# Dense products of a transformer row computed in 64-row TensorE tiles, two banks at a time, with their halves placed around the score products

## What is computed

```python
xn = layernorm(x)                                     # no affine part
q, k, v = split_heads(xn @ qkv_w + qkv_b)             # 16 heads of 16
attn = softmax(q @ k.T * 0.25)
a = (attn @ v) @ proj_w + proj_b
h = silu(xn @ wg.T) * (xn @ wu.T)                     # wg, wu: 768 x 256 integers / 127
return x + a + h @ wd.T                               # wd: 256 x 768 integers / 127
```

## Time and profile before

| | |
|---|---|
| median of 3 runs | 620.43 us (619.53 to 620.57) |
| the profiled execution | 619.78 us, of which the span from first to last instruction is 618.0 us |
| PE, busy | 599.4 us, 97% of the span |
| DVE, ACT, POOL, busy | 494.6, 372.3, 173.0 us |
| TensorE clock granted | full in all of the span's slices |

### The profile page before, as it was taken

How to read it: one execution, slowest core, us unless ns; L and a number is a source line. 1 busy time by engine, 2 the same in 40 slices (tenths; PEclk the granted TensorE clock), 3 DMA queues, 4 the chain that set the end, 5 groups by cost and what they waited for, 6 DMA issues and landing times.

```text
span 618.0 us, 10940 instructions
## 1 busy us (share of the span) xinstructions
PE 599.4 (97%) x3594; PEld 327.1 (53%) x3594; DVE 494.6 (80%) x652; ACT 372.3 (60%) x482; POOL 173.0 (28%) x181
## 2 busy tenths in 40 slices
PE   7888999999999999999999999999999999999896
PEld 6655445555555555555555455555555555554353
DVE  5898887788887887888877888878878788778752
ACT  3545765675566665766556655666657665566563
POOL 3215134220622224321342206222152212222210
PEclk9999999999999999999999999999999999999999
DMA  8680192114622176012822137221760118210201
GB/s 285 226 136 3 69 236 56 53 37 140 169 53 52 35 209 149 17 36 102 235 56 52 35 133 174 51 52 35 197 162 14 41 69 232 61 53 3 69 2 38
DMA packets 38364, 59.11 MB, mean 96 GB/s; under 512 B 6080, under 2 KB 21440, under 8 KB 38336
## 3 DMA queue, kind: packets, MB, share of 16 engines
q1 hardware_dynamic: 38336, 58.74, 35.1%
HBM read 37.23 MB, written 20.97 MB: 94 GB/s over the span
## 4 chain that ended last, share of the span: by engine, by line
PE 90%; DVE 5%; ACT 3%; issue 1%; DMA 0%; POOL 0%; DVEq 0%; ACTq 0%; POOLq 0%
PE dense L948 38%; PE o_bank L938 20%; PE st_bank L907 17%; PE s_bank L924 11%; DVE neg_max L705 2%; ACT probs L582 2%; PE dense L962 1%; PE dense L979 1%; DMA xn<-in_L_attn_x 0%; DVE gated L733 0%; DVE hid L741 0%; PE dense L1006 0%; ACT gated L621 0%; DVE w_gl L757 0%; ACT xn_th L590 0%
## 5 line engine op out<-in xcount | busy, mean ns | idle before, releaser
L582 ACT ACTIVATE probs<-st_bank 128x1024 f32<-128x1024 f32 x250 | 256.2, 1025 | 206.4 <-PE st_bank L907 202.5
L705 DVE TENSOR_REDUCE neg_max<-s_bank 128x2 f32<-128x1024 f32 x250 | 305.4, 1222 | 69.3 <-PE s_bank L924 67.2
L938 PE MATMUL o_bank<-probs,v_ones 128*32 128x512 f32 x1024 | 136.4, 604 | 0.1
L907 PE MATMUL st_bank<-q_stack,k_stack 50*128 50x512 f32 x500 | 125.0, 496 | 4.1 <-ACT probs L582 3.9
L517 POOL TENSOR_TENSOR hid_tl<-hid,hid_th 128x512 fp32r<-128x512 f32 x48 | 61.9, 1289 | 188.8 <-ACT hid_th L647 188.8
L907 PEld LDWEIGHTS st_bank<-q_stack,k_stack 50*128 50x128 f32 x500 | 46.6, 183 | 121.9 <-ACT probs L582 84.7
L924 PE MATMUL s_bank<-k_stack,q_stack 48*128 48x512 f32 x500 | 110.1, 436 | 0.7 <-DVE neg_max L705 0.7
L924 PEld LDWEIGHTS s_bank<-k_stack,q_stack 48*128 48x128 f32 x500 | 47.0, 185 | 23.1 <-DVE neg_max L705 20.8
L550 POOL TENSOR_TENSOR resid<-resid,p_bias 128x256 f32<-128x256 f32 x32 | 22.5, 735 | 101.5 <-DMA resid<-in_L_attn_x 101.5
L526 POOL TENSOR_TENSOR o_norm<-o_blocks,inv_sum 128x256 f32<-128x256 f32 x31 | 19.3, 621 | 93.7 <-DVE inv_sum L770 93.5
L938 PEld LDWEIGHTS o_bank<-probs,v_ones 128*32 128x32 f32 x1024 | 20.4, 108 | 45.8 <-issue 43.8
(11 more groups left out here) (120 smaller groups left out, 683.0 us busy)
## 6 DMA issues: line engine op xcount, KB each, us to landing
q_spread<-qk_parts SPq DMA_DIRECT2D x16, 512.0 KB, 3.2
k_spread<-qk_parts SPq DMA_DIRECT2D x16, 512.0 KB, 3.5
q_stack<-q_spread SPq DMA_DIRECT2D x64, 128.0 KB, 3.0
k_stack<-k_spread SPq DMA_DIRECT2D x64, 128.0 KB, 3.2
q_stack<-q_spread SPq DMA_DIRECT2D x64, 64.0 KB, 3.2
k_stack<-k_spread SPq DMA_DIRECT2D x64, 64.0 KB, 3.1
resid<-in_L_attn_x SPq DMA_DIRECT2D x8, 512.0 KB, 4.3
xn<-in_L_attn_x SPq DMA_DIRECT2D x7, 512.0 KB, 3.4
```

The lines of the kernel that those rows point to most:

```text
L582: nc.scalar.activation(probs[:, s % 2, 2 * half:2 * half + 2, :], transposed_bank(row, s, half)[:, :, :], ACT.Exp, scale=SCALE).then_inc(e ...
L705: nc.vector.tensor_reduce(neg_max[:, g % 2, :, NT * pair + qt], score_bank(row, half)[:, :, :], AX_X, ALU.max, negate=True).then_inc(max_d ...
L907: done = nc.tensor.matmul(transposed_bank(row, s, half)[:, r, :], k_stack[rows, pair, P * kt:P * (kt + 1)], q_stack[rows, pair, :], start= ...
L938: done = nc.tensor.matmul(o_bank[32 * j:32 * (j + 1), :], v_ones[:, kt, 8 * (g // 2) + 2 * j + g % 2, :], probs[:, (s - 1) % 2, j, :], sta ...
```

## The change

`dense` becomes one tensor of three banks, and each entry of the table names its banks. From row 0 on every dense product is cut along its contraction into array rows 0 to 63 and 64 to 127, the two row tiles that the scores use, and works on two banks: in a first half, tile 0 adds into bank A while tile 1 adds into bank B; in the second half the tiles are swapped. up and gate of one index are made together, and q and k of index 1; the others fill two banks with 256 columns each (two token tiles of v, proj and down; two halves of the tokens for q 0 and k 0). The first half of a product stands behind `scores_t` of the second pair of the step before (for up/gate one pair of matmuls ahead of `scores`, the rest behind it), the second half behind `scores_t` of the first pair of its step, or behind `scores` where it is long (down, q and k 1). The transposes (xn, max) still use the whole array.

ACT alone empties the banks of xn, q, k, up, v and max. xn, q and k go whole into a float32 tile (`whole`, on the place of `raw_d`); ACT makes the high part from there and POOL the low part. up is copied to `hid` by ACT, POOL multiplies it with the gated value, ACT and POOL split that product. The low part of the maxima is made by POOL. DVE keeps the maxima, the gate, down and proj (now two tiles of down at once). `resid` is stored and loaded in two halves. Row -1 keeps whole-array products; its last chunk is v 0 in place of gate 4.

```diff
+    (0, 0, "up", 4, 0, (2,)), (0, 0, "gate", 4, 0, (0,)),
+    (1, 0, "v", 1, 0, (1, 2)),
+    (2, 0, "up", 5, 0, (1,)), (2, 0, "gate", 5, 0, (0,)), (2, 1, "max", 1, 0, (2,)),
...
+    (5, 0, "q", 0, 1, (1, 2)),
+    (6, 0, "k", 0, 1, (0, 1)), (6, 1, "max", 2, 0, (2,)),
+    (7, 0, "proj", 1, -1, (0, 1)),
+    (8, 0, "q", 1, 1, (2,)), (8, 0, "k", 1, 1, (0,)),
+    (9, 0, "down", 0, 0, (1, 2)),
...
+    (12, 0, "up", 1, 1, (2,)), (12, 0, "gate", 1, 1, (1,)),
...
+            def half_product(spec, swap, first, last):
...
+                for n, (ready, (a, b, k)) in enumerate(terms):
+                    if not first <= n < end:
+                        continue
+                    if ready is not None and swap == 0:
+                        pe.wait_ge(*ready)
+                    for r in range(2):
+                        h = (r + swap) % 2
+                        rows = slice(HALF * r, HALF * (r + 1))
+                        done = nc.tensor.matmul(banks[h], stationary(h, a, k)[rows], moving(h, b, k)[rows],
+                                                start=swap == 0 and n == 0, stop=swap == 1 and n == len(terms) - 1,
+                                                tile_position=(HALF * r, 0))
+                return done, end == len(terms)
...
+            def end_product(row, chunk, exact):
+                pe.wait_ge(half_made, products_up_to(row, chunk))
+                done, _ = half_product(spec_of(row, chunk, exact), 1, 0, None)
+                done.then_inc(dense_done, len(made_together(row, chunk)))
...
             def step(row, exact):
                 for s in range(STEPS):
                     chunks(row, s, 0, exact)
-                    pairs(row, s, 0)
+                    here = product_at(row, s)
+                    if here and s == 0:
+                        begin_product(row, here, exact, 0)
+                    if row.has(0):
+                        scores_t(row, s, 0)
+                    if here and not long_product(here):
+                        end_product(row, here, exact)
+                    if pair_ahead(row, s, 0):
+                        scores(row, s, 0)
+                    if here and long_product(here):
+                        end_product(row, here, exact)
...
-                    if not after_scores(row, s):
-                        pairs(row, s, 1)
+                    if row.has(0) and not after_scores(row, s):
+                        scores_t(row, s, 1)
+                    ahead = product_at(row, s + 1)
+                    between = ahead and ahead[2] == "up"
+                    if between:
+                        begin_product(row, ahead, exact, 0, 1)
+                    if pair_ahead(row, s, 1):
+                        scores(row, s, 1)
+                    if ahead:
+                        begin_product(row, ahead, exact, 1 if between else 0)
...
+            def hidden_product(row, chunk):
+                m = chunk[3]
+                (up,) = [c for c in chunks_of(row.like) if c[2:4] == ("up", m)]
+                wait_freed(pool, row, up)
+                wait_freed(pool, row, chunk)
+                nc.gpsimd.tensor_tensor(gated[:, m % 2, :], gated[:, m % 2, :], hid[:, m % 2, :],
+                                        ALU.mult).then_inc(hid_product, 1)
...
+                elif kind == "up":
...
+                    nc.scalar.activation(halves(hid[:, i % 2, :]), bank, ACT.Copy,
+                                         scale=0.5 * QUANT ** 3).then_inc(act_free, 1)
...
+            def split_into_high(row, chunk, n):
...
+                nc.scalar.activation(high, whole[:, WHOLE_AT[kind, i], :], ACT.Copy).then_inc(split_high, 1)
```

More of the change, by code:

```diff
@@ L139, in rows_of, with count @@
     step(Row(ROWS, ROWS))
-PER_ROW = {kind: sum(c[2] == kind for c in STEADY) for kind in ALL}
-def count(row, kinds, chunk=None, kind=None, index=None):
+def count(row, which, chunk=None, kind=None, index=None):
     like = row.like
@@ L333, in pair_ahead, with number @@
+        def number(row, kind, index):
+            return count(row, lambda like, k: k == kind, kind=kind, index=index)
         def pair_ahead(row, step, half):
@@ L483, in step @@
                     load_stack(row, 3)
+                if row.like == ROWS:
+                    for tiles in (slice(0, 2), slice(2, 3), slice(3, 4)):
+                        sp.wait_ge(last_added, tiles.stop)
+                        sp.dma_start(out_rows[row.at - 1, :, tiles],
+                                     resid[:, tiles, :]).then_inc(out_done[tiles.start // 2], 16)
+                    sp.wait_ge(out_done[0], 16 * ROWS)
+                    sp.wait_ge(out_done[1], 16 * (ROWS + 1))
             rows_of(sp, step)
@@ new lines, in take @@
+                                                   halves(qk_parts[i][:, which, high, :].bitcast(F32)),
+                                                   ALU.add, ALU.subtract).then_inc(dve_free, 1)
+                elif kind == "gate":
+                    part = halves(gated[:, i % 2, :])
+                    nc.vector.scalar_tensor_tensor(part, part, 1.0, bank, ALU.add, ALU.mult).then_inc(dve_free, 1)
+                elif kind in ("down", "proj"):
+                    if kind == "down":
+                        dve.wait_ge(resid_ready, NT * row.at + 2 * i + 2)
+                    else:
+                        dve.wait_ge(dve_free, count(of_row(row, -1), freed_by_dve, kind="down", index=i))
@@ L867, in step @@
                             maxima(row, s, slot // 2)
+                        for chunk in chunks_at(row, s, slot):
+                            if chunk[2] in ("proj", "down"):
+                                take(row, chunk)
                         if measured and measured[0] == 0:
@@ L1062, in chunks, with long_product, product_at @@
                         sum_squares()
-            def pairs(row, s, half):
-                if row.has(0):
-                    scores_t(row, s, half)
-                if pair_ahead(row, s, half):
-                    scores(row, s, half)
+            def long_product(chunk):
+                return chunk[2] == "down" or chunk[2:4] == ("q", 1)
+            def product_at(row, s):
+                found = [c for c in products_of(row.like) if c[0] == s]
+                return found[0] if found else None
             def step(row, exact):
```

573 lines of the change are left out of this document (356 added, 217 removed), and 2 rows, old and new, of the table STEADY.

## The result

The changed kernel takes 613.25 us (median of four executions, 612.02 to 614.25) beside 620.5 for the kernel before (four, 619.53 to 624.46): ratio 0.987, 95% interval 0.9822 to 0.9918. It is faster, by 7.3 us or 1.3%. I had forecast 598.0 and a range of 589 to 612: the direction was right, two thirds of the gain are missing, and the median lies outside the range.

A forecast was written before the change was run, and what follows sets the result against it. PE was taken to bound every step, with tile-shape switches removed and half their worth lost to the st loop. From 619.8 us, less 7 x 3.0, 1.5 and 1.0, plus 1.7 for stalls, came 598.0; range 589 to 612.

The forecast's parts named there:

- priced on one row and taken seven times: Rows 0 to 6: one steady row falls from 72.2 to 69.2 us, 3.0 less, counted seven times.
- 1.5 us less for row 7: Last row, without q, k, xn or a next row: the same step-by-step arithmetic gives 1.5 us less.
- 1.0 for row -1: Row before the loop: DVE loses three multiplications of 0.67 us from its chain; between nothing and 2 us less, taken as 1.0.
- the two switches: PE's tile-shape changes into and out of each dense block: 2 x 0.19 us removed, up to 6.1 us a row.
- the st loop: From one `st_bank` matmul through ACT's exponential to the next: 1.625 us, a floor that takes half of the removed switches' worth.
- The rule of the Trainium skill on weight loads: Loads overlap matmuls only when row groups differ; as a rival, every pair costs 0.105 us more, 730 us, chance 0.02.
- Step 15: Last step of a row, with v 0: 4.04 us.
- Step 4: Step with proj 0, where q 0 must wait until DVE has added proj 0: 4.12 us.
- Steps 0, 5 and 11: Steps of a row with up/gate, q 0 and up/gate: 4.11, 3.88 and 4.21 us.
- the margin of 1.7: Added to the summed 596.3 us for stalls that a sum by steps doesn't see, about one late release a row.
- The term -3.0: Row 0, priced like a steady row: 3.0 us less.
- The fourth rival: ACT or POOL, strictly in order, releases late once or twice a row: 609 us if one, about 640 if four; chance 0.13.

The follow-up runs named there:

- e1: Changed kernel with its dense products in the whole array again, one bank after the other, the early gate/up pair moved behind `scores`: 672.67 us.
- e3: Changed kernel with each exponential over half of its columns (output not the layer's, read for time alone): 595.96 us.
- e4: Kernel before with each exponential over half of its columns (output not the layer's, read for time alone): 618.14 us.
- e2: Changed kernel with both halves of a product made together behind the scores, tile shape kept: 642.59 us.
- e8: Changed kernel with row 1 normalised by DVE in place of POOL in row 0: 608.85 us.
- e6: Changed kernel with 22 spare transposes in row 0 ahead of the wait for POOL's normalised row 1: 609.13 us.
- e5: Changed kernel with four pairs of spare matmuls behind the scores of steps 4, 5 and 7 of row 7: 610.33 us.
- e7: Changed kernel with DVE taking `o_bank` away one slot later, behind the second of two maxima: 612.77 us.
- e10: Changed kernel with row 1 normalised by DVE, spare matmuls in row 7 and v 0 in dense bank 1, all together: 606.04 us.
- e9: Changed kernel with the last product ahead of row 0 (v 0) in dense bank 1 in place of 0: 610.36 us.
- e11: Changed kernel unedited, run again on the chip of e9 and e10: 611.93 us.

## Why the prediction was wrong

**The step that failed** is the one from the steady row to the edges: "priced on one row and taken seven times", with 1.5 us less for row 7 and 1.0 for row -1. The three stretches outside the six steady rows were to give 5.5 us and took 6.6 more. In its place the runs showed a wait of 2.55 us for POOL in row 0 with a lower clock behind it, some 10 us at half clock in row 7, and a late start and a wait of 0.78 us in row -1. The mechanism of the steady rows was right; their gain was 2.4 us a row and not 3.0.

**What held.** The price of the two switches, 2 x 0.19 us a block (0.37 measured in e1); pairs 0.23 (512 columns) and 0.12 us (256) apart; the st loop at 1.62 as the new floor of the way from second to next `st`, in which about half of the switches' worth is lost (e3, e4); ACT's and POOL's new work at next to no cost in steady rows: in row 4 PE waited 0.2 us for ACT and 0.3 for DVE. e1 and e2 show that shape and place work only together: with either of them undone the kernel is slower than before. The rule of the Trainium skill on weight loads that I had weighed (page "TensorE: Matmul & The Clock Gate", Part 3) stays contradicted: dense pairs in the same two row groups follow one another by 0.23 us, with the loads of the next pair starting as the matmuls of both row groups start (322.65 and 322.66 above).

**Steady rows, 3.0 against 2.4.** Two terms of the sum were too small. Step 15, 4.04: measured 4.37 to 4.43 in rows 1 to 4 and 4.08 to 4.12 in rows 5 and 6. At the end of such a row PE starts the dense pair 0.58 us behind `s_bank`, and before its weight load the view has 0.39 us of "issue", idle time without a releaser:

```profile
329.50 0.50 PE L1094 MATMUL s_bank<-k_stack,q_stack 48*128 48x512 f32 x2
...
330.08 0.49 PE L1139 MATMUL dense<-xn_th,w_uh 64*128 64x512 f32 x1
```

There is now a product that spans the row's end, and I had taken its step for one like the others. The loop holds rows 1 to 5, so it is the four ends that lead back to the loop's start that show this; what the engine does in that idle time is not shown. Step 4, 4.12: measured 4.35, in row 6 4.17; I saw the wait for proj's add and priced it 0.2 too low. Steps 0, 5 and 11 are 0.1 longer each. In all 0.6 us in each of six rows, 3.7; the margin of 1.7 was for this.

**"Taken seven times."** This is in the first paragraph: rows 0 and 6 are within about 1% of a steady row *in the kernel before* (row 0 is 1.2% below), so I priced row 0 as one. In before PE arrived at row 1's normalise 1.0 us early, in after 2.55. A shorter PE row does not shorten the chain of statistics, moments and POOL's 4.85 us, which starts with row 0. The term -3.0 was +1.0, 4.0 us of error; e8 gives back 2.9 of it: 1.4 is the clock, which e6 gets back by filling alone, and 1.5 the wait.

**Row 7.** -1.5 was +3.5. At full clock (e5, e6, e7, e10) it is 52.0 to 52.2 against 51.9: the sum of its steps was 1.8 too good. The steps of the down products lost: the four from step 7 took 14.75 us in before (4.10, 4.10, 3.28, 3.27) and 15.56 in e10 (5.14, 5.07, 3.12, 2.23), 0.8 more; the seven ahead of them took 28.3 and 27.8 (e6), 0.5 less. The forecast had only the total of row 7, so the 1.8 can't be told apart further. The other 3.2 are the clock at 0.50 behind a stretch in which PE was busy 2.66 of 4 us. I had read the trace of before at a clock of 1.00 throughout and had no term for it.

**Row -1.** -1.0 was +2.1. I took DVE's three multiplications from its chain, but no gain from that shows on PE: its last score products of row -1 start at 45.32 in place of 44.24, 1.1 us later, of which 0.8 is there from the first dense product on (13.20, in before 12.42) and came with the weights (ACT's first take of them at 9.24, in before 8.06). The other 1.1 us come behind: PE waits 0.78 us for v 0's copy (e9 removes it), and up and gate 4 are made ahead of the first `o_bank` now, 1.86 us, where before had gate 4 alone, 1.51.

**The sum again**, in the order of the table: 3.1 + 4.0 + 3.7 + 5.0 less the 1.7 is 14.1; 612.02 less 598.0 is 14.0. The repaired kernel, 606, shows that some 6 to 7 us could be had back; the other 8 down to 598 were not had by any of these runs. The fourth rival, a release late once or twice a row, is the nearest to what happened (609 for one a row), but not its mechanism: the steady rows have none; what was met is one late release in one row, and a clock.

## What to carry to other kernels

Price a change of the bounding engine at every fixed chain that it must meet, row by row: a prologue or a last row that is "like the others" while the engine is slow may be set by another chain once it is faster. Where the engine's idle time grows, read the granted clock behind it too: "fully busy" at half clock is a loss that busy time does not show, and try cheap work in the gap: in row 0 it gave back 1.4 us in the trace of e6. A gain in one engine's work ends at the next loop; measure that loop (here 1.62 us) before counting the whole.

## What was not expected of the hardware

TensorE's granted clock fell to 0.50, the 1.2 GHz level, for about 10 us of row 7 behind a stretch of 4 us in which PE was busy 2.66. But such a stretch does not decide it alone. In the kernel before, PE was busy 2.62 of 4 us in row 7 and the clock stayed at 1.00:

```profile
577.00:581.00 4.00, 2.62 (x19) 1.00 (x17) 2.96 (x4) 2.32 (x3) 0.00 (x0) 1.00 0.01 2
```

And in e6_fill_row0, whose row 7 is the changed kernel's, the same stretch has the same busy time, and the clock holds behind it:

```profile
557.80:561.80 4.00, 2.67 (x17) 0.84 (x16) 3.71 (x5) 2.05 (x3) 0.45 (x2) 1.00 0.21 70
561.80:565.80 4.00, 3.08 (x22) 1.09 (x24) 2.51 (x3) 1.90 (x3) 0.46 (x1) 1.00 0.00 0
```

The same program of row 7 kept its clock in this trace and lost it in four (after, e8, e9, e11). Both kernels with spare matmuls in row 7 (e5, e10) had it at 1.00 there, which two traces can't tell from chance; in row 0 all five traces with the 2.55 us wait unfilled (after, e5, e7, e9, e11) took 72.4 to 73.8 us at 0.93 to 0.98, and the three with it filled or shortened (e6, e8, e10) had 1.00. What decides between two executions of one program is open; the changed kernel, unedited, was never above 0.990 in ten executions, while that of before was at 0.997 or more in most.
